# The MLP's last 64 up-projection columns as one 128-column weight of high and low part, as last but one block

## The reference

```python
# layer 1: a long convolution, then an MLP
z = rmsnorm(u, pre_norm_w) @ in_proj_w.T            # 256 -> 768
...                                                  # short conv of 3 taps, long conv, gates -> y
y = y @ out_proj_w.T + u
zm = rmsnorm(y, post_norm_w)
mlp = jax.nn.gelu(zm @ l1_w.T) * (zm @ l2_w.T) @ l3_w.T    # l1_w, l2_w: 672 x 256, l3_w: 256 x 672
return y + mlp
# layer 2: FFN 256 -> 1024 -> 256, whose weights get a rank-one sum per sequence, from tokens 1 to 16
h = jax.nn.gelu(x @ (W1 + scale * m1).T + b1, approximate=False)
out = h @ (W2 + scale * m2).T + b2
```

## Time and profile before

| | us |
|---|---|
| median of 3 runs (lowest, highest) | 1077.68 (1077.45, 1081.7) |
| the profiled execution's own time | 1076.75 |
| its span, first to last instruction | 1075.0 |
| TensorE matmul busy | 1050.8 (98%) |
| TensorE weight load busy | 1008.5 (94%) |
| VectorE busy | 877.8 (82%) |
| ScalarE busy | 710.8 (66%) |
| GpSimd busy | 299.5 (28%) |
| mean granted TensorE clock | 1.000 |

### The profile page before, as it was taken

How to read it: one execution, slowest core, us unless ns; L and a number is a source line. 1 busy time by engine, 2 the same in 40 slices (tenths; PEclk the granted TensorE clock), 3 DMA queues, 4 the chain that set the end, 5 groups by cost and what they waited for, 6 DMA issues and landing times.

```text
span 1075.0 us, 24951 instructions
## 1 busy us (share of the span) xinstructions
PE 1050.8 (98%) x9012; PEld 1008.5 (94%) x9012; DVE 877.8 (82%) x2322; ACT 710.8 (66%) x1589; POOL 299.5 (28%) x575
## 2 busy tenths in 40 slices
PE   8899999999999999999999999999999999999998
PEld 7777888899989999999999999989999999999997
DVE  7999998774788888888887878897888888887776
ACT  7879887764456666666666666656666666666644
POOL 7677775470101112111111111111112111111111
PEclk9999999999999999999999999999999999999999
DMA  3337977986322222233222222432222223222000
GB/s 130 120 117 236 294 216 196 363 318 151 83 66 41 54 57 50 52 52 58 59 60 58 52 51 60 122 96 41 60 51 50 52 53 59 59 58 60 21 21 31
DMA packets 112491, 102.83 MB, mean 96 GB/s; under 512 B 7552, under 2 KB 103744, under 8 KB 112112
## 3 DMA queue, kind: packets, MB, share of 16 engines
q1 hardware_dynamic: 111136, 98.67, 36.2%
q0 software_dynamic: 736, 2.51, 0.6%
q10 hardware_dynamic: 496, 0.05, 0.0%
HBM read 75.75 MB, written 30.70 MB: 99 GB/s over the span
## 4 chain that ended last, share of the span: by engine, by line
PE 67%; DVE 6%; issue 2%; ACT 1%; POOL 0%; POOLq 0%; DVEq 0%; ACTq 0%
PE ps_ring L1551 35%; PE ps_w L1551 16%; PE ps_m L1551 9%; PE ps_o L1551 4%; PE ps_rt L1566 2%; DVE base L1373 1%; PE ps_w L1561 1%; DVE bn L1277 1%; PE ps_m L1617 1%; DVE prod L1320 0%; DVE ht_l L1289 0%; DVE pt_l L1289 0%; POOL sc L1129 0%; ACT rows L1254 0%; DVE yrow L1512 0%
## 5 line engine op out<-in xcount | busy, mean ns | idle before, releaser
L1129 POOL TENSOR_TENSOR sc<-sc,small 128x2 f32<-128x2 f32 x127 | 94.5, 744 | 676.8 <-DVE sc L1501 404.6
L1194 ACT ACTIVATE gate<-ps_ring 128x256 f32<-128x256 f32 x192 | 73.0, 381 | 129.7 <-PE ps_ring L1551 128.9
L1215 ACT ACTIVATE hid<-ps_ring,small 128x256 f32<-128x256 f32 x256 | 112.1, 483 | 24.2 <-PE ps_w L1551 13.4
L1551 PE MATMUL ps_ring<-mt_l,wl_h 128*128 128x256 f32 x640 | 125.5, 277 | 2.6 <-DVE mt_l L1289 2.6
L1551 PE MATMUL ps_ring<-mt_h,wl_h 128*128 128x256 f32 x640 | 125.5, 277 | 1.8 <-DVE prod L1320 1.3
L1551 PE MATMUL ps_ring<-mt_h,wl_l 128*128 128x256 f32 x640 | 124.9, 277 | 0.0
L1289 DVE TENSOR_TENSOR ht_l<-hid,ht_h 128x256 fp32r<-128x256 f32 x256 | 103.1, 423 | 16.5 <-ACT ht_h L1219 10.6
L1551 PE MATMUL ps_ring<-xt_h,we_h 128*128 128x256 f32 x512 | 104.8, 285 | 2.5 <-DVE prod L1320 2.4
L1551 PE MATMUL ps_ring<-xt_h,we_l 128*128 128x256 f32 x512 | 101.3, 279 | 0.0
L1551 PE MATMUL ps_ring<-xt_l,we_h 128*128 128x256 f32 x512 | 101.3, 279 | 0.0
L1320 DVE TENSOR_TENSOR prod<-ps_ring,gate 128x256 f32<-128x256 f32 x192 | 80.7, 420 | 24.2 <-ACT gate L1194 20.6
(11 more groups left out here) (203 smaller groups left out, 2720.2 us busy)
## 6 DMA issues: line engine op xcount, KB each, us to landing
toep_scratch<-taps_scratch SPq DMA_DIRECT2D x26, 512.0 KB, 7.4
toep<-toep_scratch SPq DMA_DIRECT2D x26, 512.0 KB, 8.8
xa<-in_x SPq DMA_DIRECT2D x16, 512.0 KB, 4.9
x_scratch<-x2c SPq DMA_DIRECT2D x16, 512.0 KB, 3.7
x2s<-x_scratch SPq DMA_DIRECT2D x32, 256.0 KB, 6.7
xa_c<-in_x SPq DMA_DIRECT2D x32, 256.0 KB, 2.7
xb_c<-in_x SPq DMA_DIRECT2D x32, 256.0 KB, 2.7
yin<-seq SPq DMA_DIRECT2D x124, 64.0 KB, 5.5
```

The costliest lines, as they stand in the source:

```text
L1129: nc.gpsimd.tensor_tensor(sc[:, to], sc[:, to], neg_half[:, 0, 0:CC], ALU.pow).then_inc(S[done], 1)
L1194: nc.scalar.activation(gate[rows_of, m % 2], ring[m % RING][rows_of, 0], ACT.Gelu_apprx_tanh).then_inc(S["gate_done"], 1)
L1215: nc.scalar.activation(hid[:, m % HIDS], block_of, ACT.Gelu, bias=b1s[:, m:m + 1]).then_inc(S["hid_done"], 1)
L1551: mm = nc.tensor.matmul(out, lhs(a, kk), rhs(b, kk), start=(j == 0), stop=(closed and j == len(todo) - 1))
```

## The change

The rest's 64 columns get one weight tile of 128 columns: the high parts of l2 and l1, then the low parts. Two matmuls with all 128 columns on the high part of the tokens give high times high in rows 0 to 63 and low times high in rows 64 to 127. Two more, with the first 64 columns on the low part of the tokens, add to rows 0 to 63. So there are 4 matmuls for 6. The two halves of the rows are added on VectorE: ScalarE copies rows 64 to 127 to `gate`, VectorE adds rows 0 to 63 from PSUM to it, ScalarE takes the gelu of rows 32 to 63 in place, and VectorE multiplies rows 0 to 31 with 32 to 63. The rest becomes block m = 4, and the last full block is m = 5.

```diff
-        wrest = [sb(whole, f"wrest_{s}", [P, KB, 2 * REST], F32R) for s in "hl"]
+        wrest = sb(whole, "wrest", [P, KB, 4 * REST], F32R)
...
-                         (raw[:, k, :, FULL * P:], [w[:, :, at:at + REST] for w in wrest]))
+                         (raw[:, k, :, FULL * P:], [wrest[:, :, i:i + REST] for i in (at, 2 * REST + at)]))
...
+    REST_AT = FB - 2
...
+        def full_block(m):
+
+            return m - (m > REST_AT)
...
-            if m < FULL:
-                return pt[0][:, m], prod[:, m % 2], pt[1][:, m]
+            if m != REST_AT:
+                return pt[0][:, full_block(m)], prod[:, m % 2], pt[1][:, full_block(m)]
...
-                rows_of = slice(0, P) if m < FULL else slice(REST, 2 * REST)
-                nc.scalar.activation(gate[rows_of, m % 2], ring[m % RING][rows_of, 0],
-                                     ACT.Gelu_apprx_tanh).then_inc(S["gate_done"], 1)
+                opened, source = gate[:, m % 2], ring[m % RING][:, 0]
+                if m == REST_AT:
+                    nc.scalar.activation(opened[2 * REST:], source[2 * REST:], ACT.Copy).then_inc(S["rest_low"], 1)
+                    product_high(n, m - 1)
+                    act.wait_ge(S["rest_done"], n + 1)
+                    opened = source = opened[REST:2 * REST]
+                nc.scalar.activation(opened, source, ACT.Gelu_apprx_tanh).then_inc(S["gate_done"], 1)
...
-                        if 0 < m < FB - 1:
+                        if 0 < m < REST_AT:
                             product_high(n, m - 1)
...
                 b = FB * n + m
+                wait(dve, S["pl_done"], b - 1)
+                if m == REST_AT:
+                    rest_sum(n)
+                    product_low(n, m - 1)
                 dve.wait_ge(S["gate_done"], b + 1)
-                wait(dve, S["pl_done"], b - 1)
-                if m < FULL:
+                if m != REST_AT:
                     value, gated = ring[m % RING][:, 1], gate[:, m % 2]
                 else:
-                    value, gated = ring[m % RING][0:REST, 0], gate[REST:2 * REST, m % 2]
+                    value, gated = gate[0:REST, m % 2], gate[REST:2 * REST, m % 2]
                 nc.vector.tensor_tensor(product_views(m)[1], value, gated, ALU.mult
                                         ).then_inc(S["prod_done"], 1)
-                if m > 0:
+                if 0 < m != REST_AT:
                     product_low(n, m - 1)
                 if m == FB - 1:
                     product_low(n, m)
+
+            def rest_sum(n):
+
+                pair = gate[:, REST_AT % 2]
+                dve.wait_ge(S["rest_low"], n + 1)
+                nc.vector.tensor_tensor(pair[0:2 * REST], ring[REST_AT % RING][0:2 * REST, 0], pair[2 * REST:], ALU.add
+                                        ).then_inc(S["rest_done"], 1)
...
-                if m == FULL:
+                if m == REST_AT:
                     nc.vector.tensor_copy(pstack[REST:2 * REST], src).then_inc(S["stacked"], 1)
...
-                if m < FULL:
+                if m != REST_AT:
                     for side, w in enumerate((wl1, wl2)):
-                        mm = product(bank[:, side], lambda a, kk: w[a][:, kk, m * P:(m + 1) * P],
+                        mm = product(bank[:, side], lambda a, kk: w[a][:, kk, chunk(full_block(m))],
...
                 else:
-                    mm = product(bank[0:2 * REST, 0], lambda a, kk: wrest[a][:, kk],
-                                 lambda b, kk: zt[b][:, kk], KB)
+                    for b, columns in enumerate((4 * REST, 2 * REST)):
+                        for kk in range(KB):
+                            mm = nc.tensor.matmul(bank[0:columns, 0], wrest[:, kk, 0:columns], zt[b][:, kk],
+                                                  start=(b == kk == 0), stop=(b == kk == 1),
+                                                  skip_group_check=True)
```

More of the change, by code:

```diff
@@ L1009, in phase_c @@
                    xhat_done yrow_done
-                   squared rms_arg rms_done zm_done zt_mm zh_done zl_done ml_mm gate_done prod_done
+                   squared rms_arg rms_done zm_done zt_mm zh_done zl_done ml_mm rest_low rest_done gate_done prod_done
                    ph_done high_here pl_done stacked m_mm a_done a_stat a_var a_scale a_mean x1_done x_stat x_var
```

## The result

The changed kernel takes 1089.73 us (median of 4 runs, 1088.53 to 1090.15); the kernel before, run beside it, took 1078.91 (1077.45 to 1081.7). The ratio is 1.0095, with an interval of 1.0071 to 1.012: slower by 10.8 us. Forecast were 1084.0, with a range from 1075 to 1087.5. Medians are of all executions of a run; the ratios leave out three disturbed executions (one each of e3, e4 and e5, of 1733, 1155 and 4796 us).

A forecast was written before the change was run, and what follows sets the result against it. TensorE was taken to bound the repeating steps, VectorE steps 0 to 3 and 17 to 19. Losses of 4.0 there and 2.6 in repeating steps made 6.6 us slower: 1083.4 from 1076.75, 1084.0 on the median's footing, range 1075 to 1087.5.

The forecast's parts named there:

- What is removed: On TensorE in a repeating step, 4 matmuls for 6 save 0.227 us; 5.7 over 25 steps.
- The chain beside TensorE: Copy, sum and gelus on ScalarE and VectorE make the table load 0.60 us later; up-projection block 4 stalls on `hid`.
- Neighbours on shifted rows: Copy, sum and the rest's gelu don't overlap their neighbours on ScalarE and VectorE, giving the delay of 0.60 us.
- Steps 0, 1 and 17 to 19: VectorE as chain: 0.45 us longer each in steps 0 and 1; 0.6 in 17, 1.02 in 18, 0.27 in 19.
- Steps 2 and 3: Step 2: VectorE's first FFN low part 1.02 us later, gelus waiting for the sum; step 3: 0.27 longer at block 5.
- the repeating step's sum: The two matmuls' gain is gone to late `hid`, a stalled start costs more: step 0.10 us longer, 2.6 over 25.
- The rival of the slower pace: MLP matmuls go at the FFN's 0.118 us distance, not 0.113: 0.3 a step, 7 more, 1091; chance 0.08.
- move addresses only: Edits of `full_block`, the weight's layout and GpSimd's split lie outside the path: cost zero.
- the rival of overlapping neighbours: Neighbours overlap on shifted rows too: delay 0.38 us, step some 0.02 shorter, 3.0 on at seams, 1080.2; chance 0.22.
- the bounds above it: Repeating step by ScalarE's delay: with 0.38 us it is 0.12 shorter than before, with 0.7 it is 0.2 longer.

The follow-up runs named there:

- e3: As e2, with the last full block's gelu and product ahead of the rest's; 1084.04 us, ratio 1.0045 to the kernel before.
- e4: The changed kernel with the rest as second block of five, everything computed; 1081.33 us, ratio 1.0037 to the kernel before.
- e5: The kernel before with four of the rest's six matmuls, leaving out low weight x high tokens; 1071.51 us, ratio 0.9953.
- e10: e1 with the rest last, as before the change; low weight x high tokens left out; 1071.22 us, ratio 0.994.
- e1: The changed kernel without copy and sum, gelu and product reading PSUM, low weight x high tokens left out; 1079.43 us, ratio 1.0019.
- e2: The changed kernel with FFN up-projection block 2 waiting for the sum instead of the rest's product; 1087.17 us, ratio 1.0095.
- e7: The changed kernel with the rest's second pass run twice, so six matmuls; 1087.4 us, ratio 1.0097.
- e9: The kernel before with only the order changed: rest as block 4 of 5, old weights, six matmuls; 1083.21 us, ratio 1.0054.
- e6: e1 with the rest's second pass run twice, so six matmuls; 1083.32 us, ratio 1.005.
- e8: e4 with one matmul of the rest repeated, so five matmuls; 1082.88 us, ratio 1.0054.
- e11: The kernel before with its two rest weights side by side in one tile; 1077.29 us, ratio 1.0001.
- e12: e9 with one unread matmul, 64 columns wide, and a wait added behind the last block; 1111.33 us, ratio 1.0306.
- e13: e9 with one unread matmul, 128 columns wide, and a wait added behind the last block; 1114.0 us, ratio 1.0327.
- e14: The kernel before with one unread matmul, 128 columns wide, added behind its rest; 1088.2 us, ratio 1.0102.

## Why the prediction was right and wrong, by its steps

- **What is removed: right.** 0.227 a step was forecast; e5 and e10 give 24.54 - 24.31 = 0.23.
- **The chain beside TensorE: right in place, a little high in size.** The table load, the stall at block 4 and its releaser came as said. Forecast were 0.33 a step (the saved 0.23 given back, and 0.10 more); the change less e1 is 24.77 - 24.52 = 0.25, both without their odd steps (two of 25.55 and 25.71, and one of 25.12). By stages, the FFN's up-projection is 0.29 longer than in e1 (0.10 of it the start behind the stall); the MLP is 0.03 longer and out- and down-projection 0.06 shorter on average, since they are at the slower pace in other steps than in e1.
- **Neighbours on shifted rows: right.** The copy ends at 511.40 and the high part starts at 511.43; the sum starts at 511.69 and the low part at 512.14, 0.45 later for 0.42 of length. The rule of the Trainium skill for VectorE (VectorE: DVE Perf Modes, "Two Vector instructions with no wait between them") held for the sum and the rest's product. The overlap of 93 ns between activations that the Trainium skill states (ScalarE: Activation LUTs, "What ACT_TABLE_LOAD costs") is not there behind the 32-row gelu: it ends at 512.56, the next starts at 512.59.
- **Steps 0, 1 and 17 to 19: right for 1, and for 17 to 19 together.** Step 0 is 0.75 longer (forecast 0.45), step 1 0.43 (0.45), steps 17 to 19 1.94 (1.9).
- **Steps 2 and 3: too low.** Step 2 was 1.98 longer, not 1.0: about half of it is the fall of the clock. In e2 and e7 the clock stays up in step 2, and that step is 0.96 longer than before; e7 has the same stall as the change (1.93) there. That the longer stall brought the fall is not shown: the stall of 1.90 in step 18 did not, and in e1 and e10 the clock fell in step 18 behind stalls of 1.01 and 0.90, while in e9 (1.01) and before (0.90) it did not. Step 3 is 0.55 longer, not 0.27. I had priced the delay, but not a fall of the clock.
- **The step that failed** is the repeating step's sum, in the term that it left out: the same matmuls at the same distance. The forecast said a repeating step is 0.10 longer (2.4 over the 24); it is 0.23 longer without the two odd steps, and the 24 together are 7.2 longer with them. The rival of the slower pace named the right thing, "if the MLP's go at the slower one", and gave it 0.3 in each step and a chance of 0.08. It took the MLP in one step of three (0.28) and parts of the FFN, the out- and the down-projection in others (0.03 to 0.14 each). e9 measures it by itself: 24.76 for 24.54 (without one odd step of 25.05), **0.22 us a step**, from the order alone, which I had costed at zero ("move addresses only"). With the stacked weight it is e1 less e5, 24.52 - 24.31 = 0.21, or 5.0 over the 24. That this rival's total, 1091, lies near the measured 1089.7 is in part luck: the pace brought 5.0 of its 7, and the odd steps and the clock much of the rest.
- **A sum of the prediction that is wrong:** the rival of overlapping neighbours takes a step as 0.02 shorter, but the bounds above it have 0.12 for the same delay of 0.38, the start's 0.10 included. The rival takes it off twice; its 1080.2 should be some 2.5 lower.
- **Not forecast:** two repeating steps are about 0.9 longer. In both the last norm waits 1.05 for GpSimd's `shift`, where in the other repeating steps it waits 0.18 at most (before 0.11). `shift` is made by three small operations, which take 2.02 from start to end in these two steps and 1.1 to 1.3 in the others (1.28 from 532.61 to 533.89):

```profile
557.34 1.02 POOL L1151 TENSOR_TENSOR shift<-mvf,sc 128x2 f32<-128x2 f32 x1
558.43 0.19 POOL L1154 TENSOR_TENSOR shift<-shift,mean_a 128x2 f32<-128x2 f32 x1
558.71 0.65 POOL L1157 TENSOR_TENSOR shift<-shift,small 128x2 f32<-128x2 f32 x1
```

So the account of the 12.9 us: -5.4 for two matmuls less in 24 steps, +5.9 for the chain, +5.0 for the pace, +1.7 for the two odd steps, and +5.7 for steps 0 to 3 and 17 to 19, of which some 1.0 is the clock. The forecast's span was 1081.6, so it is 6.3 short: 4.6 in the repeating steps and 1.7 in the others.

What stays open: why the order changes TensorE's pace. Shown is that it does (e9), and that the number of matmuls (e6 to e8), the layout (e11) and the stacked weight with the rest last (e10) don't. Not shown is whether it is the order itself or the width of the last load ahead of the transposes, which the new order makes 128. The pace changes mostly at the border of stages and does not go with the granted clock (1.00 throughout). That the moment of arrival at such a border decides would fit e12 to e14, and fits badly with the same cycle at four, five and six matmuls. Open too are why GpSimd's `shift` takes longer in two steps, and what decides whether the clock falls behind a stall.

## What to carry to other kernels

Where TensorE is the whole chain, two matmuls less were a gain with the old order of its blocks (e5, e10) and none with the new one (e1); a reorder is itself an edit with a price, to be measured alone (here 0.22 us a step, as much as was to be saved). Before adding an operation ahead of an activation-table change, measure how much later that may be: here there was slack for less than 0.4 us, and 1.06 us more on that chain cost 0.78. At seams where another engine is the chain keep the old form. Before a step's length is compared, look at its granted clock: a fall cost 1.0 here, and did not come with every stall of its length.

## What the runs showed of the hardware

- TensorE runs the same matmul (128x128 weight, 256 columns, weight load between each) at one of two distances, 0.113 or 0.118 us, mostly for a stage at a time, with a granted clock of 1.00 in both. 24 FFN matmuls take 2.74 or 2.83, the MLP's 66 take 7.49 or 7.77, the 12 of the out-projection 1.37 or 1.41.
- A stall does not as a rule end the slower pace: in the change's up-projection the distance is 0.118 ahead of the stall at block 4 in 23 of the 24 repeating steps, and behind it too in 20; in the other four it is 0.113 for about half of the 24 matmuls.
- After a stall of 1.91 us (step 2 of the change) the clock fell to 1.2 GHz 1.4 us after TensorE had started again, and stayed there for some 3.4 us. Behind a stall of 1.90 in step 18 of the same execution, and of 1.93 in step 2 of e7, it did not fall; behind 1.01 (e1) and 0.90 (e10) in step 18 it did. The kernel before has mean granted clocks from 0.994 to 1.000 over its executions, of 1080.6 us at the lowest and 1075.7 to 1078.2 at the highest.
- The same three GpSimd operations of 128x2 took 1.1 to 1.3 us in most steps of the change and 2.02 in two, by the profile's times; one by one 0.41, 0.52 and 0.19, or 1.02, 0.19 and 0.65.
